# Full attention on one core: query and key projected by features and stacked by transfers in SBUF, scores of two heads on the two halves of the array

## What is computed

```
xn  = layernorm(x)
qkv = xn @ w_qkv.T                        # 512 x 768 for each batch
q, k, v = split(qkv); q, k = rope(q), rope(k)        # 16 heads of 16
scores = q @ k.T / sqrt(16)               # per head 512 x 512
out = softmax(scores) @ v                 # per head 512 x 16
attn = out @ w_out.T
```

## Time and profile before

| | us |
|---|---|
| median of 3 executions | 4979.3 (4978.19 to 4979.38) |
| span of the profiled execution | 4976.4 |
| first store of attn_res (batch 0) issued | 156.26 |
| store of batch 14 | 1321.57 |
| store of batch 15, the last | 1384.75 |

### The profile page before, as it was taken

One profiled execution on the slowest core, in us unless ns is written; L12 is line 12 of the kernel. 1 busy time (PEld: TensorE's weight loads), 2 busy tenths in 40 slices (PEclk: granted clock), 3 DMA queues, 4 the chain that ended last, 5 costly groups with the idle time before them and its releaser, 6 DMA issues.

```text
span 4976.4 us, 86488 instructions
## 1 busy us (share of the span) xinstructions
PE 4105.8 (83%) x30816; PEld 2420.5 (49%) x30816; DVE 3737.6 (75%) x6579; ACT 2470.1 (50%) x2841; POOL 1445.1 (29%) x1467
## 2 busy tenths in 40 slices
PE   6888888888847888888888888667888888888888
PEld 3333333333335555555555555444555555555555
DVE  7787878788755777777788787367777777777784
ACT  3555555555624455545455545334454555454454
POOL 1000000000023334434344333133343444343442
PEclk9999999999968999999999999778999999999999
DMA  0000000000010000000000000200000000000000
GB/s 27 22 18 23 19 23 18 23 18 22 10 57 16 20 29 19 19 23 24 23 25 19 19 27 15 68 16 12 19 27 20 28 19 19 26 20 24 24 19 19
DMA packets 122499, 114.37 MB, mean 23 GB/s; under 512 B 9372, under 2 KB 121040, under 8 KB 122320
## 3 DMA queue, kind: packets, MB, share of 16 engines
q1 hardware_dynamic: 122320, 111.95, 7.3%
HBM read 69.74 MB, written 33.55 MB: 21 GB/s over the span
## 4 chain that ended last, share of the span: by engine, by line
issue 24%; PE 20%; POOL 13%; DVE 12%; ACT 2%; SPq 0%; DMA 0%; POOLq 0%; DVEq 0%
PE f_p L979 4%; POOL f_hT_l L1362 4%; DVE f_rn L233 3%; POOL f_u L1350 3%; POOL f_u L1347 3%; PE f_p L1015 3%; PE f_p L990 2%; PE f_p L925 2%; DVE f_bt L1216 2%; DVE f_ss L1206 2%; PE f_p L1037 1%; PE f_p L998 1%; PE f_p L965 1%; PE f_p L966 1%; PE f_p L909 1%
## 5 line engine op out<-in xcount | busy, mean ns | idle before, releaser
L652 DVE TENSOR_REDUCE m_negm<-m_p 128x2 f16<-128x1024 f32 x512 | 602.1, 1225 | 159.5 <-PE m_p L438 157.9
L540 ACT ACTIVATE m_Pr<-m_p 128x1024 f32<-128x1024 f32 x512 | 497.3, 1020 | 228.7 <-PE m_p L454 222.7
L1347 POOL TENSOR_TENSOR f_u<-f_u,f_bt 128x1024 f32<-128x1024 f32 x128 | 300.5, 2348 | 933.9 <-DVE f_bt L1216 933.9
L1236 DVE TENSOR_REDUCE f_negm<-f_p 128x4 bf16<-128x1024 f32 x256 | 297.4, 1225 | 194.4 <-PE f_p L947 193.4
L694 POOL TENSOR_TENSOR m_rc<-m_rc,m_rs 128x512 f32<-128x512 f32 x64 | 84.9, 1326 | 1189.6 <-DVE m_rs L617 1189.6
L1037 PE MATMUL f_p<-f_xhT_h,f_w_h 128*128 128x512 f16 (+1 forms) x768 | 325.7, 424 | 70.6 <-DVE f_hp L1307 70.6
L438 PE MATMUL m_p<-m_KT,m_QT 128*128 128x512 f16 x1024 | 281.2, 382 | 65.8 <-DVE m_negm L652 29.5
L454 PE MATMUL m_p<-m_QT,m_KT 128*128 128x512 f16 x1024 | 276.8, 382 | 58.3 <-DVE m_negm L652 33.0
L1362 POOL TENSOR_TENSOR f_hT_l<-f_hp,f_hT_h 128x512 f16<-128x512 f32 x192 | 235.5, 1227 | 304.3 <-ACT f_hp L1135 304.2
L1350 POOL TENSOR_TENSOR f_u<-f_u,f_rn 128x1024 f32<-128x1024 f32 x128 | 249.4, 1949 | 256.0 <-DVE f_rn L237 256.0
L1037 PE MATMUL f_p<-f_xhT_h,f_w_l 128*128 128x512 f16 (+1 forms) x768 | 323.2, 421 | 0.0
(11 more groups left out here) (233 smaller groups left out, 10587.5 us busy)
## 6 DMA issues: line engine op xcount, KB each, us to landing
f_xs<-out SPq DMA_DIRECT2D x32, 512.0 KB, 4.2
f_xr<-out SPq DMA_DIRECT2D x32, 512.0 KB, 4.0
f_ar<-attn_res SPq DMA_DIRECT2D x32, 512.0 KB, 5.0
out<-f_xb SPq DMA_DIRECT2D x32, 512.0 KB, 3.2
m_xin<-in_L_attn_x SPq DMA_DIRECT2D x16, 512.0 KB, 4.3
out<-m_xn SPq DMA_DIRECT2D x16, 512.0 KB, 3.0
attn_res<-m_res SPq DMA_DIRECT2D x16, 512.0 KB, 3.2
f_x1s<-f_x SPq DMA_DIRECT2D x32, 254.0 KB
```

The lines of the kernel that those rows point to most:

```text
L540: act.activation(Pr[kt % 2][:, 2 * u:2 * u + 2, :].rearrange("p h t -> p (h t)"), psum[w.slot("M2", g, kt, u)][:, :], ACT.Exp).then_inc(*w ...
L652: dve.tensor_reduce(negm[:, 2 * u:2 * u + 2, h], psum[w.slot("M1", h, u)][:, :].rearrange("p (a k) -> p a k", a=2), AX.X, ALU.max, negate= ...
L1236: dve.tensor_reduce(negm[:, :, h], psum[w.slot("L1", h)][:, :].rearrange("p (n k) -> p n k", n=NT), AX.X, ALU.max, negate=True).then_inc(* ...
L1347: pool.tensor_tensor(u[r][:], u[r][:], bt[:], ALU.add).then_inc(*bt_used.up(I))
```

## The change

- wq's columns for query and key are reordered on the host (_head_halves): the first halves of all heads' features, then the second halves. The step PQ,i (i = 0 query, 1 key) projects with the weights as the stationary operand, so that features lie on partitions and tokens in columns: 24 matmuls of 512 columns into one PSUM tile. DVE multiplies the tile by cosine and by sine in two instructions of 128 x 1024; POOL adds them.
- SP,i: ACT makes the high half hi (128 x 1024), POOL subtracts to get lo. SS and MS go away, with stack_ready, kv_ready and qT_ready.
- ST: SP issues 24 transfers of 64 KB within SBUF (8 x 8 x 512 fp16 at the destination) that lay hi and lo into QT and KT: three parts, [high, low, high] against [high, high, low], of 16 rows for each head, even heads from partition 0, odd ones from partition 64. PE's M1 waits for all 24 (stacked).
- PV: the value is projected apart (24 matmuls of 256 columns), and ACT copies it in one instruction (before in four).
- M1 and M2: a tile of two matmuls now holds two heads, one on rows 0 to 47 of the array, one on rows 64 to 111 (M2 one row more). The number of tiles, their size and the number of matmuls stay.
- MM: two transfers in place of one.
- The order of steps changes for the batch ahead; the setup clears less and loads larger tables.

The diff, cut to the parts that the prediction speaks of:

```diff
@@ -300,11 +302,11 @@
 
 
     order = """T.M2,3,0 B.M1,0 T.M2,3,1 B.M1,1 T.MV,3,0 T.MV,3,1 T.M2,3,2 B.M1,2 T.MV,3,2 T.M2,3,3 B.M1,3 T.MV,3,3 B.M1,4
-               B.MM,0 T.MO,3 B.M1,5 T.MT B.M1,6 T.MP B.M2,0,0 B.M1,7 B.MV,0,0 B.M2,0,1 B.M1,8 A.LX B.MM,1 B.M2,0,2 B.MV,0,1
-               A.LN,0 B.M2,0,3 B.MV,0,2 B.M1,9 B.M2,1,0 A.LN,1 B.M1,10 A.LN,2 B.MV,0,3 A.LS B.M2,1,1 B.MV,1,0 B.M1,11 B.MO,0
-               A.XT B.M2,1,2 B.MV,1,1 B.M1,12 B.MM,2 A.MQ,0 B.M2,1,3 B.MV,1,2 B.M1,13 B.MV,1,3 B.M1,14 A.MQ,1 B.M2,2,0 B.MO,1
-               B.M2,2,1 A.SS,0 A.MQ,2 A.SS,1 B.MV,2,0 A.MS,0 B.M1,15 A.MQ,3 B.M2,2,2 A.SS,2 A.MS,1 A.SS,3 B.MV,2,1 B.MM,3
-               B.M2,2,3 A.MS,2 B.MV,2,2 B.MV,2,3 A.MS,3 B.MO,2"""
+               B.MM,0 T.MO,3 B.M1,5 T.MT B.M1,6 T.MP A.LX B.M2,0,0 B.M1,7 B.MV,0,0 B.M2,0,1 B.M1,8 A.LN,0
+               B.MM,1 B.M2,0,2 B.MV,0,1 A.LN,1 B.M2,0,3 B.MV,0,2 B.M1,9 A.LN,2 A.LS A.XT B.M2,1,0 B.MV,0,3 B.M1,10 A.PQ,0
+               B.M2,1,1 B.MV,1,0 B.MO,0 B.M1,11 A.PQ,1 B.M2,1,2 B.MV,1,1 A.SP,0 B.M1,12 B.MM,2 A.PV B.M2,1,3 B.MV,1,2 A.SP,1
+               A.ST B.M1,13 B.MV,1,3 B.M1,14 B.M2,2,0 B.MO,1 B.M2,2,1 B.MV,2,0 B.M1,15 B.M2,2,2 B.MV,2,1 B.MM,3 B.M2,2,3
+               B.MV,2,2 B.MV,2,3 B.MO,2"""
 
     order = " ".join(f"{w},0 {w},1" if w[2:4] in ("M1", "M2", "MV") else w for w in order.split())
...
-        QT, KT = [[sb(f"{n}{p}", [P, H, T], F16) for p in range(2)] for n in ("QT", "KT")]
+        rc, rs = [[sb(f"{n}{r}", [P, 2, T], F32) for r in range(2)] for n in ("rc", "rs")]
+        hi, lo = [[sb(f"{n}{r}", [P, 2, T], F16) for r in range(2)] for n in ("hi", "lo")]
+        QT, KT = [[sb(f"{n}{p}", [P, NP2, T], F16) for p in range(2)] for n in ("QT", "KT")]
         vm = [sb(f"vm{p}", [P, NT, H, VW], F32) for p in range(2)]
-        negm, mT = sb("negm", [P, NT, H], F16), sb("mT", [HG, T], F16)
...
@@ -410,49 +411,50 @@
                                           xn[:, t, c * P:(c + 1) * P], identf[:])
                 mm.then_inc(*w.fills("XT"))
 
-            def mq(I, t):
-                w.wait(w.is_drained("XT"), w.is_free("MQ", t))
-                ps = psum[w.slot("MQ", t)]
-                for n0, n1 in ((0, 2 * D), (2 * D, 3 * D)):
+            def pq(I, i):
+                w.wait(w.is_drained("XT"), w.is_free("PQ", i))
+                for half in range(2):
+                    n0 = i * D + half * P
+                    for c in range(NC):
+                        for k, (a_, b_) in enumerate(((wq_h, xT_h), (wq_l, xT_h), (wq_h, xT_l))):
+                            mm = pe.matmul(psum[w.slot("PQ", i)][:, half * T:(half + 1) * T], a_[:, c, n0:n0 + P], b_[:, c, :],
+                                           start=(c == 0 and k == 0), stop=(c == NC - 1 and k == 2))
+                mm.then_inc(*w.fills("PQ", i))
+
+            def pv(I):
+                pe.wait_ge(*w.is_free("PV"))
+                for t in range(NT):
                     for c in range(NC):
                         for k, (a_, b_) in enumerate(((xT_h, wq_h), (xT_h, wq_l), (xT_l, wq_h))):
-                            mm = pe.matmul(ps[:, n0:n1], a_[:, c, t * P:(t + 1) * P], b_[:, c, n0:n1],
-                                           start=(c == 0 and k == 0), stop=(c == NC - 1 and k == 2))
-                mm.then_inc(*w.fills("MQ", t))
-
-            def ms(I, t):
-                pe.wait_ge(*stack_ready.at(I, t + 1))
-                for key, st in (("MSk", kst), ("MSq", qst)):
-                    pe.wait_ge(*w.is_free(key, t))
-                    ps = psum[w.slot(key, t)][:, :].bitcast(F16)
-                    for h in range(H):
-                        mm = pe.transpose(ps[0:4 * DH + 1, h * P:(h + 1) * P], st[t % 2][:, h, 0:4 * DH + 1], ident[:])
-                    mm.then_inc(*w.fills(key, t))
+                            mm = pe.matmul(psum[w.slot("PV")][:, t * D:(t + 1) * D], a_[:, c, t * P:(t + 1) * P],
+                                           b_[:, c, 2 * D:3 * D], start=(c == 0 and k == 0), stop=(c == NC - 1 and k == 2))
+                mm.then_inc(*w.fills("PV"))
 
             def m1(I, h, u):
-                pe.wait_ge(*kv_ready.at(I, 1))
-                pe.wait_ge(*qT_ready.at(I, 1))
+                pe.wait_ge(*stacked.at(I, stacked.per))
                 pe.wait_ge(*w.is_free("M1", h, u))
-                for v in range(2):
-                    t = 2 * u + v
-                    mm = pe.matmul(psum[w.slot("M1", h, u)][:, v * T:(v + 1) * T],
-                                   QT[I.par][:, h, t * P:(t + 1) * P], KT[I.par][:, h, :], start=True, stop=True)
+                pr, t = h // 2, 2 * (h % 2) + u
+                for e in range(2):
+                    mm = pe.matmul(psum[w.slot("M1", h, u)][:, e * T:(e + 1) * T],
+                                   QT[I.par][e * S:e * S + KR, pr, t * P:(t + 1) * P], KT[I.par][e * S:e * S + KR, pr, :],
+                                   start=True, stop=True)
                 mm.then_inc(*w.fills("M1", h, u))
 
             def mmax(I, g):
                 w.wait(w.is_drained("M1", (g + 1) * HG - 1, NT // 2 - 1), w.is_free("MM", g))
                 ps = psum[w.slot("MM", g)][:, :].bitcast(F16)
                 for t in range(NT):
-                    mm = pe.transpose(ps[0:HG, t * P:(t + 1) * P], negm[:, t, g * HG:(g + 1) * HG], ident[:])
+                    mm = pe.transpose(ps[0:HG, t * P:(t + 1) * P], negm[:, t, g].rearrange("p e u -> p (e u)"), ident[:])
                 mm.then_inc(*w.fills("MM", g))
 
             def m2(I, g, kt, u):
-                pe.wait_ge(*mrow_done.at(I, 16 * (g + 1)))
+                pe.wait_ge(*mrow_done.at(I, 32 * (g + 1)))
                 pe.wait_ge(*w.is_free("M2", g, kt, u))
-                for v in range(2):
-                    h = g * HG + 2 * u + v
-                    mm = pe.matmul(psum[w.slot("M2", g, kt, u)][:, v * T:(v + 1) * T],
-                                   KT[I.par][:, h, kt * P:(kt + 1) * P], QT[I.par][:, h, :], start=True, stop=True)
+                pr = g * HG // 2 + u
+                for e in range(2):
+                    rows = slice(e * S, e * S + KR + 1)
+                    mm = pe.matmul(psum[w.slot("M2", g, kt, u)][:, e * T:(e + 1) * T],
+                                   KT[I.par][rows, pr, kt * P:(kt + 1) * P], QT[I.par][rows, pr, :], start=True, stop=True)
                 mm.then_inc(*w.fills("M2", g, kt, u))
...
-            def mq(I, t):
-                act.wait_ge(*w.is_full("MQ", t))
-                act.activation(vm[I.par][:, t, :, 0:DH],
-                               psum[w.slot("MQ", t)][:, 2 * D:3 * D].rearrange("p (h d) -> p h d", h=H),
-                               ACT.Copy, scale=1 / WSCALE).then_inc(*w.frees("MQ", t))
-
-            def ms(I, t):
-                act.wait_ge(*w.is_full("MSk", t))
-                act.activation(KT[I.par][0:4 * DH + 1, :, t * P:(t + 1) * P],
-                               psum[w.slot("MSk", t)][:, :].bitcast(F16)[0:4 * DH + 1, :].rearrange("p (h t) -> p h t", h=H),
-                               ACT.Copy).then_inc(*w.frees("MSk", t))
-                if t == NT - 1:
-                    act.activation(mark_a[:], mark_in[:], ACT.Copy).then_inc(*kv_ready.up(I))
+            def pv(I):
+                act.wait_ge(*w.is_full("PV"))
+                act.activation(vm[I.par][:, :, :, 0:DH], psum[w.slot("PV")][:, :].rearrange("p (t h d) -> p t h d", t=NT, h=H),
+                               ACT.Copy, scale=1 / WSCALE).then_inc(*w.frees("PV"))
+
+            def sp_(I, i):
+                act.wait_ge(*summed.at(I, i + 1))
+                act.wait_ge(*stacked.before(I, 1))
+                act.activation(hi[i][:], rc[i][:], ACT.Copy).then_inc(*hi_ready.up(I))
...
@@ -607,49 +605,18 @@
                                   xT_h[:].rearrange("p c t -> p (c t)"), ALU.subtract)\
                     .then_inc(*w.frees("XT"))
...
-
-            def ss(I, t):
-                r = t % 2
-                dve.wait_ge(*summed.at(I, t + 1))
...
-                if t == NT - 1:
-                    dve.memset(mark_v[:], 0.0).then_inc(*qT_ready.up(I))
+            def pq(I, i):
+                dve.wait_ge(*w.is_full("PQ", i))
+                if not I.first:
+                    dve.wait_ge(*lo_ready.before(I, 1))
+                ps = psum[w.slot("PQ", i)][:, :].rearrange("p (s t) -> p s t", s=2)
+                dve.tensor_tensor(rc[i][:], ps, cos_t[:].unsqueeze(1).to_broadcast([P, 2, T]), ALU.mult)
+                dve.tensor_tensor(rs[i][:], ps[:, ::-1, :], sin_t[:], ALU.mult).then_inc(*w.frees("PQ", i))
 
             def m1(I, h, u):
                 dve.wait_ge(*w.is_full("M1", h, u))
-                dve.tensor_reduce(negm[:, 2 * u:2 * u + 2, h], psum[w.slot("M1", h, u)][:, :].rearrange("p (a k) -> p a k", a=2),
+                pr, t = h // 2, 2 * (h % 2) + u
+                dve.tensor_reduce(negm[:, t, pr // 2, :, pr % 2], psum[w.slot("M1", h, u)][:, :].rearrange("p (a k) -> p a k", a=2),
```

(32 more changed lines are left out.)

108 lines of the change are left out of this document (39 added, 69 removed).

## The result

The changed kernel takes 5070.6 us (median of 4 runs, 5069.0 to 5072.3) against 4978.7 us for the kernel before (4974.0 to 4979.4): ratio 1.0186, 95% interval 1.0171 to 1.0200. It is 1.9% slower, 92 us; 4863 was forecast, in a range of 4785 to 4960. Rival B, "the transfers are the bound", is what happened. "ratio" is always a kernel's time over that of the kernel before, measured beside it.

The account below looks back on a forecast made before the run. It took coupling between engines, none full, as the bound: round 72.9 + 0.4 + 1.1 + 1.3 = 75.7 us against 83.2. Saving 116 us in all gave 4860, plus 2.9 to the median: 4863, range 4785 to 4960.

Parts of the forecast that it names:

- Rival B: SP's queue and its DMA engines: stack transfers bound the round; 5260 us at two engines; slower 10%, mild form 6%.
- 24 make 12.0 ... and a 64 KB transfer lands 2.1 after issue: Stack transfers on SP: 0.5 us issue each from 57.9, issued by 69.9, landed at 72.0 us of the round.
- signs that the prediction set for B: SP's issue of a stack transfer over 0.8 us, and PE's M1,0 waiting for stacked.
- The start: Before the rounds: PQ, POOL, ACT and 24 transfers run bare in place of MQ, SS and MS, about 1 us more.
- The walk: One round traced from M2,3,0 at t = 0 in four legs, to 72.9 us before transfers, clock and loop jump.
- Leg 1: From M2,3,0 to the tail's residual on DVE: four score, exponential and value steps, then MT and MP, ending at 23.9 us.
- Leg 2: From the residual to xn on DVE, through M1 reductions and LayerNorm, ending at 37.4 us; PE waits 5.2 us.
- Leg 3: From xn through the transposes of x and PQ to the key's products on DVE, ending at 52.8 us.
- Leg 4: From the key's products to the round's end, by ACT: copies, exponentials, four score steps, MO,2, ending at 72.9 us.
- rival A: Score tiles on PE: the array's row halves do not overlap, 3.3 us a round, 4913 us; 14%.
- I take 1.1, bounds 0 and 3.7: Half clock behind the 5.2 us stall ahead of XT slows XT and perhaps PQ,0: 1.1 us a round.
- Rival C: PE's clock: thinned work holds 1.2 GHz for most of the round, some 17 us a round, 5130 us; 5%.

Follow-up runs that it names:

- e1: Kernel before with eleven blocks of bare transfers added: 0.98 us a transfer to eight neighbouring rows, 0.60 to 0.64 for blocks 1 and 2, rows 6 and 16 apart.
- e2: Changed kernel with each stack transfer writing 8 rows six apart instead of 8 neighbouring ones: 4974.3 us, ratio 0.9998.
- e9: Changed kernel with rows six apart, later transposes of x, high halves issued first and the last four transfers behind the last maxima: 4943.0 us, ratio 0.9921.
- e11: e3 with 22 idle products on TensorE ahead of the wait for the transposes of x: 4901.8 us, ratio 0.9850.
- e3: Changed kernel moving only the first of the stack's three parts, 8 of 24 transfers a round: 4939.1 us, ratio 0.9917.
- e13: e9 with two M2 steps and MV ahead of the first M1, and the transposes back in the changed kernel's place: 4943.2 us, ratio 0.9935.
- e14: e13 with 22 idle products ahead of the wait for the transposes' input: 4913.9 us, ratio 0.9868.
- e12: Changed kernel with 22 idle products ahead of the transposes and 40 ahead of the wait for the last maxima: 5083.4 us, ratio 1.0214.
- e7: Changed kernel with the stack built through DRAM, 4 stores and 8 loads instead of 24 transfers, order untouched: 5075.7 us, ratio 1.0195.
- e15: e13 with the transposes of x later and 10 idle products ahead of them: 4955.1 us, ratio 0.9955.

## Why the prediction was wrong

**The term that failed** is "24 make 12.0 ... and a 64 KB transfer lands 2.1 after issue". It took its price from rows of issue and of a single landing, and treated 24 transfers in a row as if only their issue queued. Issue was 0.66 instead of 0.5 (15.9 us in all), and the drain 0.98 a transfer. In the mean of 14 rounds M2,3,0 starts 24.7 us behind the stack's first issue, forecast 15.4 (57.9 to 73.3): 9.3 of the 12.8 us by which a round is too long. The other 3.5 lie ahead of the stack: 63.8 us from M2,3,0 to its first issue, where 57.9 and 2.4 for clock and jump were forecast. The prediction's own formula for B, round = 57.9 + 24 x + 2.1 + 1.1 + 2.4, gives 87.0 with x = 0.98; measured were 88.5. It had "reaches 83.2 at x = 0.82" and gave that 10%. Its argument against B was sound as far as it went (eight engines, not one) and answered the wrong question: it asked how many engines read, not where they write. e1 and e2 show that the eight rows at the writing end did it: 5.9 us a round and, in the bare start, 12 us more (first store at 184.1 against 171.7 in e2). At the store of batch 14 that is 14 x 5.87 + 12.4 = 94.6 of e2's 96 us. The signs that the prediction set for B did not show it: SP's issue was 0.66, not over 0.8, and it was M2,3,0 that waited, for the maxima queued behind the stack, not M1,0. The start, forecast 1 us longer, was 28 longer; e2 takes 12 of them away, e9, with later transposes and another order of issue, 9 more (162.4 against 171.7); the rest is open.

**The walk**, for the round from M2,3,0 at 593.12 to the next at 684.30 (91.2 us, a long one). DVE's ends of the legs:

```profile
622.25 1.23 DVE L642 SCALAR_TENSOR_TENSOR m_res<-m_p,m_xin 128x1024 f32<-128x1024 f32 x1 [2.40 <-PE m_p L491]
...
635.67 1.37 DVE L599 TENSOR_SCALAR m_xn<-m_xin,m_mv,m_rstd 128x256 f32<-128x256 f32 x4
...
652.57 1.22 DVE L614 TENSOR_TENSOR m_rs<-m_p,m_sin 128x1024 f32<-128x1024 f32 x1
```

- Leg 1: 30.4 instead of 23.9. TensorE was at half clock until 603 (granted 0.50 over 593 to 603) and mostly again from 618 (0.57 over 618 to 622); 16 value matmuls took 3.64, and the last 15 of MP's 24 started 0.21 apart instead of 0.11.
- Leg 2: 13.6, forecast 13.5. The stall ahead of XT is where it was put: 5.27 us at 637.18, forecast 5.2.
- Leg 3: 16.7, forecast 15.4, the transposes at half clock (1.97 us). Leg 4, to the last output copy's reader at 674.3: 20.5, forecast 20.1.
- Then the wait: 10.07 us, forecast 0.4.

**The halves of the array overlap**, as taken (rival A is out). One tile of two matmuls and its reader at full clock, to set beside the earlier trace rows:

```profile
661.86 0.38 PE L456 MATMUL m_p<-m_QT,m_KT 49*128 49x512 f16 x2
...
662.28 1.02 ACT L538 ACTIVATE m_Pr<-m_p 128x1024 f32<-128x1024 f32 x1 [0.15 <-PE m_p L456]
```

ACT follows after 0.42 (0.64 before, 0.45 forecast).

**The clock** was the second mis-sized term: "I take 1.1, bounds 0 and 3.7". e11 against e3 shows 2.5 us a round for the stall ahead of XT alone, within the bounds; but half clock reaches further than one stall, as leg 1 shows. (The row it took the half clock from reads 0.87 for 1440 to 1445 us and 0.50 only for 1450 to 1455.) Rival C expected half clock for most of the round, and the mean of 0.84 is short of that. With the stack cheap, filling that one stall is worth 29 us, e13 against e14. What it costs in the changed kernel e12 can't say, but the 2.4 us a round that it won ahead of the stack speak for a price of that size there too.

**What is left open.** e11, with little stack and nearly the full clock, still takes 77.3 us a round and not 75.7 less the 1.1 for the clock. Most of it lies in leg 1: from M2,3,0 to the store of the tail e11 takes 27.9 us in the mean of 14 rounds (29.3 in the changed kernel), where the walk has the residual at 23.9. TensorE's waits for tiles are longer there than the walk's rules allow (M2 behind m_negm is 26 us over the phase in e3), but no run takes that apart.

## What to carry to other kernels

Price a chain of transfers by its drain as well as its issue: ask how many partitions the writing end touches and how far apart they are, and how many DMA engines the outermost size allows; either can be the limit, and DMA share against GB/s tells which (0.58 at 67 GB/s in the changed kernel: engines held up; 0.20 at 80 in e7: too few engines). If a layout's row order is free, as the order of a contraction is, interleave the rows so that each transfer spreads; it is a change of a slice's step. And taking work off an engine that others wait with can lower its clock: see which gaps it opens before counting the work as time. Idle products in such a gap give it back only where they end no later than the wait (e11 and e14, not e12 and e15).

## What was not expected of the hardware

- Transfers of 64 KB from 64 partitions to eight neighbouring ones run at 67 to 71 GB/s; to eight rows six or sixteen apart they go as fast as SP issues, 100 GB/s and more. Eight neighbouring rows filled from DRAM took 82.
- A transfer of 64 partitions x 1 KB takes SP 0.62 to 0.67 us to issue alone and 0.66 in the kernel, where loads of eight rows of 6 KB from DRAM took 0.34.
- 4.9 us of idle products a round made the kernel 37 us faster (e3 to e11) at a clock of 0.94 instead of 0.87.
